# A transformer block with a feed-forward layer: both first feed-forward products as two row tiles between the score pairs, the output projection in chunks of four

## The reference

```
def _ada_rmsnorm(x, t, gamma_w, beta_w):
    return gamma * _rmsnorm(x) + beta          # gamma, beta: t @ weights, one row per sequence
def _attention(x, W_q, W_k, W_v, W_o):         # 16 heads, d_head = 16, scale = 1/4
    attn = softmax(scale * einsum('bnqd,bnkd->bnqk', q, k))
    return einsum('bnqk,bnkd->bnqd', attn, v) ... @ W_o.T
def _swiglu(x, gate_w, hidden_w, out_w, out_b):
    return silu(x @ gate_w.T) * (x @ hidden_w.T) @ out_w.T + out_b
x = x + a_alpha * _attention(_ada_rmsnorm(x, ...), ...)
x = x + f_alpha * _swiglu(_ada_rmsnorm(x, ...), ...)
out = ((x - mean) * rsqrt(var + eps) * weight + bias + tanh(convInfo @ lin_w.T + lin_b)) * weight + bias
```

## Time and profile before

| | |
|---|---|
| median of 3 runs | 820.65 us (817.95 to 827.77) |
| the profiled execution | 820.58 us, of which the span of the trace is 818.6 us |
| mean granted clock of TensorE | 0.971 of full speed (2.4 GHz) |
| busy: PE, PEld | 743.4 us (91%), 489.4 us |
| busy: DVE, ACT, POOL | 536.4 us (66%), 479.0 us (59%), 386.1 us (47%) |
| DMA | 100.15 MB, 122 GB/s in the mean |

### The profile page before, as it was taken

The page is one execution under the profiler, slowest core; times in us unless marked ns, Lnnn a source line. Parts: engine busy times, 40 slices in busy tenths (PEclk is TensorE's granted clock), DMA queues, the critical chain, the costliest instruction groups (busy, mean ns, idle before and its releaser), DMA issues.

```text
span 818.6 us, 14287 instructions
## 1 busy us (share of the span) xinstructions
PE 743.4 (91%) x5110; PEld 489.4 (60%) x5110; DVE 536.4 (66%) x777; ACT 479.0 (59%) x854; POOL 386.1 (47%) x489
## 2 busy tenths in 40 slices
PE   4767878899999999899998999899998999999896
PEld 3423333356666667566766666666675666569895
DVE  3576676667667776667666776667666677526586
ACT  3346666666656665667566666567546565663332
POOL 3234341533246542657147453656337443674753
PEclk9769999899999999999999999999999999999898
DMA  6756385244422544054421644243430630022010
GB/s 184 256 196 205 122 255 176 89 169 131 168 80 88 198 108 154 30 181 137 152 91 39 218 111 141 79 151 123 143 118 17 193 114 33 29 65 81 14 27 26
DMA packets 60670, 100.15 MB, mean 122 GB/s; under 512 B 9424, under 2 KB 17032, under 8 KB 60600
## 3 DMA queue, kind: packets, MB, share of 16 engines
q1 hardware_dynamic: 59928, 98.52, 37.6%
q10 hardware_dynamic: 544, 0.52, 0.2%
q0 software_dynamic: 128, 0.20, 0.1%
HBM read 59.60 MB, written 39.09 MB: 121 GB/s over the span
## 4 chain that ended last, share of the span: by engine, by line
PE 70%; DVE 8%; DMA 6%; issue 6%; ACT 5%; POOL 3%; SPq 1%; POOLq 0%; ACTq 0%; DVEq 0%
PE ps_x L1176 15%; PE ps_o L1156 11%; PE ps_s L1143 11%; PE ps_j L1073 11%; PE ps_x L1191 9%; PE ps_m L1128 7%; DVE mx L904 3%; ACT prob L739 3%; DMA qs<-m_hl 2%; PE ps_j L1111 1%; POOL fx L517 1%; PE ps_m L1176 1%; DVE sc L915 1%; DMA stack_scratch<-qk_lo 1%; PE ps_s L1176 1%
## 5 line engine op out<-in xcount | busy, mean ns | idle before, releaser
L904 DVE TENSOR_REDUCE mx<-ps_m 128x2 f32<-128x1024 f32 x222 | 271.8, 1224 | 88.2 <-PE ps_m L1128 83.0
L739 ACT ACTIVATE prob<-ps_s 128x1024 f32<-128x1024 f32 x256 | 262.0, 1024 | 114.6 <-PE ps_s L1143 114.0
L1143 PE MATMUL ps_s<-qs,ks 64*128 64x512 f32 x512 | 129.5, 502 | 22.3 <-ACT prob L739 12.6
L1143 PEld LDWEIGHTS ps_s<-qs,ks 64*128 64x128 f32 x512 | 48.3, 185 | 155.1 <-ACT prob L739 128.6
L1156 PE MATMUL ps_o<-prob,v 128*32 128x512 f32 x1024 | 138.3, 613 | 0.0
L482 POOL TENSOR_TENSOR a_lo<-act_y,a_hi 128x256 fp32r<-128x256 f32 x100 | 73.2, 732 | 137.0 <-ACT a_hi L771 136.4
L1176 PE MATMUL ps_x<-n_hi,gh_hi 128*128 128x256 f32 x436 | 127.3, 292 | 0.0
L1176 PE MATMUL ps_x<-n_hi,gh_lo 128*128 128x256 f32 x436 | 122.0, 280 | 0.0
L1176 PE MATMUL ps_x<-n_lo,gh_hi 128*128 128x256 f32 x436 | 121.8, 279 | 0.0
L1128 PE MATMUL ps_m<-ks,qs 64*128 64x512 f32 x444 | 100.7, 450 | 10.1 <-DVE mx L904 7.5
L764 ACT ACTIVATE gate_t<-ps_x 128x256 f32<-128x256 f32 x109 | 41.9, 384 | 93.8 <-PE ps_x L1176 93.6
(11 more groups left out here) (158 smaller groups left out, 1310.3 us busy)
## 6 DMA issues: line engine op xcount, KB each, us to landing
qs<-stack_scratch SPq DMA_DIRECT2D x32, 512.0 KB, 4.1
ks<-stack_scratch SPq DMA_DIRECT2D x32, 512.0 KB, 5.0
stack_scratch<-qk_hi SPq DMA_DIRECT2D x60, 256.0 KB, 3.2
out_scratch<-o_raw SPq DMA_DIRECT2D x32, 256.0 KB, 2.4
stack_scratch<-qk_lo SPq DMA_DIRECT2D x30, 256.0 KB, 3.6
xa<-in_x SPq DMA_DIRECT2D x8, 512.0 KB, 4.0
o_c<-out_scratch SPq DMA_DIRECT2D x16, 256.0 KB
d_c<-reciprocal_scratch SPq DMA_DIRECT2D x16, 256.0 KB
```

The costliest lines, as they stand in the source:

```text
L739: act.activation(prob[:, n % 2, 2 * h:2 * h + 2, :], ps_s[:], ACT.Exp, scale=SCALE).then_inc(p_r, 1)
L904: dve.tensor_reduce(mx[:, group % 2, :, h, qt], max_pair(mp)[:], AX.X, ALU.max).then_inc(mx_red, 1)
L1143: mm = pe.matmul(ps_s[:, s, :], ks[r:r + 64, g, j, kb * P:(kb + 1) * P], qs[r:r + 64, g, j, :], start=True, stop=True)
```

## The change

PE's order in units 28 to 127 becomes: `scores(n, 0)`, `max_scores`, `gate_hidden(e)`, `scores(n, 1)`, `max_scores`, `attend(n - 1)`, in every fourth unit a chunk, `job(n)`.

- `gate_hidden(e)` is now 24 matmuls over 64 rows and 256 columns, in twelve pairs. In a pair the upper half of the rows works for the gate channels and the lower half for the hidden channels; they write the two banks of `ps_x`. The gate weights lie in partitions 0 to 63 and the hidden weights in partitions 64 to 127 (the loads of the weights are split accordingly). Since each half of the rows must see all 256 inputs, the inputs are stored a second time with the halves of the partitions swapped (`n2_x`); SP copies them with two DMAs for each half sequence (`swap_halves`), and the seventh pair waits for them.
- `project_out` is no longer run in every unit: `project_chunk` does four values of e in a row (24 matmuls) into `ps_j`, in slots 2, 6, 10 and 14 from unit 34 on, 24 chunks in all. DVE scales each chunk and POOL adds it: twice per half sequence instead of once. The buffers of the activations grow from 4 to 6 (`RING`), and `gate_t` and `act_y` shrink by one each.
- In the units with a chunk the MT job goes to `ps_x[:, 0]` and not to `ps_j`. The next `gate_hidden` waits for its evacuation (`m_lo_r`).
- V and K change places in `SCHEDULE`. `qk_hi` and `qk_lo` have one buffer each and not two, and some of SP's issues move by one slot.
- ACT does `tanh(e)` before the second exponentials. DVE does `gate(e)` behind the two reductions, then the scaling of the chunk, then the evacuation of the job.
- In the tail PE does two `gate_hidden` and then two `project_out`, where it alternated. The products of 32 values of e are left for the tail there, and were 30.

The core of the diff:

```diff
--- before.py
+++ after.py
-SCHEDULE = (("TR", 1, 1), ("FT", 1, -2), ("MT", 1, 0), ("Q", 0, 1), ("K", 0, 1), ("V", 0, 1), ("MT", 2, 0), ("WO", 0, -1),
-            ("WO", 1, -1), ("FT", 0, -1), ("MT", 3, 0), ("Q", 1, 1), ("K", 1, 1), ("V", 1, 1), ("MT", 0, 1),
+SCHEDULE = (("TR", 1, 1), ("FT", 1, -2), ("MT", 1, 0), ("Q", 0, 1), ("V", 0, 1), ("K", 0, 1), ("MT", 2, 0), ("WO", 0, -1),
+            ("WO", 1, -1), ("FT", 0, -1), ("MT", 3, 0), ("Q", 1, 1), ("V", 1, 1), ("K", 1, 1), ("MT", 0, 1),
...
+CH = 4
+CHUNKS = TAIL // JC * JC // CH
+CHUNK_AT = GH_AT + CH + LAG
+RING = 6
+def chunk_at(n):
+
+    c = (n - CHUNK_AT) // CH
+    return c if n >= CHUNK_AT and (n - CHUNK_AT) % CH == 0 and c < CHUNKS else None
...
+        n2 = sb("n2", [P, 2, 2, KC, HT], F32R)
+        n2_x = sb("n2_x", [P, 2, 2, KC, HT], F32R)
+        gate_t = sb("gate_t", [P, HT])
...
-        ps_f = ps_x[:, 1].rearrange("p (t n) -> p t n", t=2)
+        ps_f = ps_o[:].rearrange("p (t n) -> p t n", t=2)
+        ps_c = ps_j[:].rearrange("p (t n) -> p t n", t=2)
...
+        def gh_banks(e):
+
+            return ps_x if e < TAIL else (ps_m, ps_x, ps_s)[(e - TAIL) % 3]
...
+        def mt_bank(n):
+
+            return ps_j if chunk_at(n) is None else ps_g
...
+            def swap_halves(b, h):
+
+                hf = 2 * b + h
+                sp.wait_ge(n2_lo_r, 2 * (hf + 1))
+                if b > 0:
+                    sp.wait_ge(gh_full, JC * (hf - 1))
+                for r in range(2):
+                    sp.dma_start(n2_x[64 * r:64 * r + 64, h].bitcast(F32), n2[64 - 64 * r:128 - 64 * r, h].bitcast(F32))\
+                      .then_inc(n2_x_in[h], 16)
...
             def gate_hidden(e):
 
-                hf, j, bank = e // JC, e % JC, gh_bank(e)
-                user = gh_bank_user(e)
-                if user is not None:
-                    pe.wait_ge(y_r, user + 1)
-                if e >= TAIL:
-                    pe.wait_ge(p_r, 2 * NU)
-                    pe.wait_ge(mx_red, 2 * NU)
+                hf, j, bank = e // JC, e % JC, gh_banks(e)
+                h = hf % 2
+                if gh_user(e) is not None:
+                    pe.wait_ge(y_r, gh_user(e) + 1)
                 if j == 0:
                     pe.wait_ge(n2_lo_r, 2 * (hf + 1))
                 if e == 0:
                     pe.wait_ge(piece_lo, PIECES)
                     pe.wait_ge(mx_red, 2 * (GH_AT + LEAD))
+                if e == TAIL:
+                    pe.wait_ge(p_r, 2 * NU)
+                    pe.wait_ge(mx_red, 2 * NU)
+                mt = job_at(e + GH_AT - 1)
+                if chunk_at(e + GH_AT - 1) is not None and mt:
+                    pe.wait_ge(m_lo_r, NG * mt[2] + mt[1] + 1)
                 for m in range(12):
-                    i, k, (a, c) = m // 6, m // 3 % 2, PARTS[m % 3]
-                    mm = pe.matmul(bank[:, HT * i:HT * (i + 1)], GH[a][:, k, i, j * P:(j + 1) * P], N2[c][:, hf % 2, k, :],
-                                   start=(m % 6 == 0), stop=(m % 6 == 5), skip_group_check=True)
+                    x, k, (a, c) = m // 6, m // 3 % 2, PARTS[m % 3]
+                    if m == 6 and j == 0:
+                        pe.wait_ge(n2_x_in[h], 32 * (hf // 2 + 1))
+                    for r in range(2):
+                        rows = slice(64 * r, 64 * r + 64)
+                        mm = pe.matmul(bank[:, r, 0:HT], GH[a][rows, 2 * k + (r ^ x), j * P:(j + 1) * P],
+                                       N2[x][rows, h, c, k, :], start=(m == 0), stop=(m == 11))
                 mm.then_inc(gh_full, 1)
...
+            def project_chunk(c):
+
+                job_evacuated(last[0])
+                for e in range(CH * c, CH * c + CH):
+                    project_out(e, ps_c, e == CH * c, e == CH * c + CH - 1)
+                last[0] = ("F", c)
...
+            def middle_unit(n):
+                scores(n, 0)
                 if n + LEAD < NU:
                     max_scores(2 * (n + LEAD))
-                if 0 < n <= NU:
-                    attend(n - 1)
-                if n < NU:
-                    scores(n, 1)
+                gate_hidden(n - GH_AT)
+                scores(n, 1)
                 if n + LEAD < NU:
                     max_scores(2 * (n + LEAD) + 1)
-                if n < NU:
-                    job(n)
-                if 0 <= e < NE:
-                    gate_hidden(e)
-                if 0 <= e - LAG < NE:
-                    project_out(e - LAG)
-                if n >= NU:
-                    job(n)
-
-            for n in range(LAST):
-                unit(n)
-
+                attend(n - 1)
+                if chunk_at(n) is not None:
+                    project_chunk(chunk_at(n))
+                job(n)
+
+            def tail_units(n):
+                e = n - GH_AT
+                for d in range(2):
+                    if e + d < NE:
+                        gate_hidden(e + d)
+                if n == NU:
+                    attend(n - 1)
+                job(n)
+                for d in range(CHUNKS * CH if n == NU else e - 2, e):
+                    if d < NE:
+                        project_tail(d)
+                job(n + 1)
```

More of the change, by code:

```diff
@@ L139, in build @@
         y_f = fx[:]
+        n2_hi, n2_lo = n2[:, :, 0], n2[:, :, 1]
+        first_hi, first_lo = (n2[:, :, i].rearrange("p h k n -> p h (k n)") for i in range(2))
+        zeros = sc[:].rearrange("p t n -> p (t n)")
         ps_s = ps("ps_s", [P, 2, T])
@@ L1186, in project_out, with project_tail, run @@
                     pe.wait_ge(a_tail_r, e - TAIL + 1)
-                if j == 0 and hf > 0:
-                    pe.wait_ge(sc_r, SC_NO["F", hf - 1])
                 for t in range(2):
                     for m, (a, c) in enumerate(PARTS):
-                        mm = pe.matmul(ps_f[:, t, :], A[a][:, e % 4, t * P:(t + 1) * P], OW[c][:, j, :],
-                                       start=(j == 0 and m == 0 and t == 0), stop=(j == JC - 1 and m == 2),
-                                       skip_group_check=True)
+                        mm = pe.matmul(out[:, t, :], A[a][:, e % RING, t * P:(t + 1) * P], OW[c][:, j, :],
+                                       start=(first and m == 0 and t == 0), stop=(end and m == 2), skip_group_check=True)
                 mm.then_inc(f_done, 1)
-            def run(job):
+            def project_chunk(c):
[3 more added lines that the diff above has]
+                last[0] = ("F", c)
+            def project_tail(e):
+                hf, j = e // JC, e % JC
+                if j == 0:
+                    if CH * CHUNKS == e:
+                        pe.wait_ge(o_r, NG * B)
+                    else:
+                        pe.wait_ge(sc_r, SC_NO["H", hf - 1])
+                project_out(e, ps_f, j == 0, j == JC - 1)
+            def run(job, n):
                 kind, i, b = job
@@ L1254, in job, with early_unit @@
             def job(n):
-                if job_at(n):
+                if job_at(n) and mt_bank(n) is ps_j:
                     job_evacuated(last[0])
-                    run(job_at(n))
+                    run(job_at(n), n)
                     last[0] = job_at(n)
-            def unit(n):
-                e = n - GH_AT
-                if n < NU:
-                    scores(n, 0)
+                elif job_at(n):
+                    pe.wait_ge(s_r, n - GH_AT + 1)
+                    run(job_at(n), n)
+            def early_unit(n):
+                scores(n, 0)
+                max_scores(2 * (n + LEAD))
+                if n > 0:
+                    attend(n - 1)
+                scores(n, 1)
+                max_scores(2 * (n + LEAD) + 1)
+                job(n)
+            def middle_unit(n):
+                scores(n, 0)
                 if n + LEAD < NU:
                     max_scores(2 * (n + LEAD))
-                if 0 < n <= NU:
-                    attend(n - 1)
-                if n < NU:
-                    scores(n, 1)
+                gate_hidden(n - GH_AT)
+                scores(n, 1)
                 if n + LEAD < NU:
                     max_scores(2 * (n + LEAD) + 1)
-                if n < NU:
-                    job(n)
-                if 0 <= e < NE:
-                    gate_hidden(e)
-                if 0 <= e - LAG < NE:
-                    project_out(e - LAG)
-                if n >= NU:
-                    job(n)
-            for n in range(LAST):
-                unit(n)
+                attend(n - 1)
+                if chunk_at(n) is not None:
+                    project_chunk(chunk_at(n))
[6 more added lines that the diff above has]
+                if n == NU:
+                    attend(n - 1)
+                job(n)
+                for d in range(CHUNKS * CH if n == NU else e - 2, e):
+                    if d < NE:
+                        project_tail(d)
+                job(n + 1)
+            for n in range(GH_AT):
+                early_unit(n)
+            for n in range(GH_AT, NU):
+                middle_unit(n)
```

(2 more changed lines are left out.)

277 lines of the change are left out of this document (151 added, 126 removed).

## The result

The changed kernel takes 865.7 us in the median (864.42 to 865.92, 4 runs) against 823.2 of the kernel before on the same chip: a ratio of 1.054 (1.050 to 1.058), slower. The span of its profiled execution is 863.8 us, against 818.6.

What follows compares the result with a forecast made beforehand. PE was taken to bound units 28 to 121. To 820.6 us were added 17 for those units, 12 for the tail and 1 for units 0 to 27, giving 850, with a range of 806 to 871.

Steps and rivals of the forecast that it cites:

- PE's own work, 89 to 84.1 a block, and the waits, 12.3: Block of 16 units: PE's work falls from 89 to 84.1 us, waits come to 12.3, so 96.4 against 92.7.
- my list: Waits of one block summed by the kind of job before them: 13.3 us, taken as 12.3.
- Units 28 to 121, +17: Large stage: +3.7 us a block gives +21.7 over 94 units, less 4.5 for first six units without chunks.
- Units 0 to 27, +1: Start of the kernel: same order, but K one unit later and more DMA issues, +1 us.
- Halved `qk_hi`, 0, at worst 1 a block: Q and K evacuations: a write lands in 3.2 us, two units lie between, so 0, at worst 1 us per block.
- The last six units, 0: Units 122 to 127: no max_scores, so no reduction to wait for; the groups come to the same 26 us.
- The tail, +12: Tail: tiling changes 5.6 us, two more project_out 1.4, waits for the swapped copy 5; bounds 3 and 18.
- rival 1: Large stage: evacuations behind the job stay hidden, waits stay at 3.5 us a block, 799 us, faster; chance 0.13.
- w: The waits in a block, in us, in the forecast's formula for the whole change.
- 2: Large stage: waits are about two thirds of the sum, one hiding in another, 804 to 837 us; chance 0.24.
- 3, the clock: FT in each block: granted clock falls, 7 us at half clock cost 3.4, times six, 870 us; chance 0.08.
- 4, pairs that show their loads: gate_hidden's twelve pairs: each load shows, 0.10 us, so 1.2 more per gate_hidden, about 940 us; chance 0.05.

Runs made afterwards that it cites:

- x_dve: Changed kernel, but in units 28 to 127 DVE evacuates TR, Q, K and FT jobs and takes statistics after the next unit's first reduction; 841.6 us, 1.026.
- x_job: Changed kernel with the job ahead of attend in units without a chunk, DVE's order as it was; 834.1 us, ratio 1.013.
- x_rows: Changed kernel, but SP issues the rows of the maxima ahead of the read of the stack in slots 6 and 14; 854.3 us, ratio 1.038.
- x_sched: Changed kernel with Q, K, V in the order of the kernel before; 887.9 us, ratio 1.082.
- x_full: Changed kernel with gate_hidden as twelve matmuls over all 128 rows in the same place, which changes the computation; 870.5 us, ratio 1.063.
- x_full2: x_best2 with gate_hidden as twelve matmuls over all 128 rows in the same place, which changes the computation; 832.5 us, ratio 1.015.
- x_best2: Changed kernel with DVE's and ACT's evacuations and side work deferred into the next unit, rows of maxima first on SP, chunk scaled late; 810.0 us, 0.984.

## Why the prediction was right

Direction, range and main mechanism held: 850 was forecast with 806 to 871, and 865.7 came, near the upper end of the range. The mechanism, evacuations that lost their cover and stand ahead of a reduction, is what x_dve and x_job show; x_dve puts it at 26.5 of the 45.2 us. Several sums came out well because two errors in them cancel, and that is luck. By its steps, on the profiled executions (818.6 to 863.8, +45.2; forecast +29 or 30):

- **PE's own work, 89 to 84.1 a block, and the waits, 12.3.** Means over the units 34 to 121 give 96.8 us for a block with four chunks (forecast 96.4), of which about 11.0 are waits (how much later a group starts than without a wait; as idle time the profile has 7.6 a block): 1.7 behind the TR jobs (2.7 in my list), 1.1 and 2.0 behind the FT jobs (1.1 and 2.2), 2.0 behind Q and K (2.8), 0.3 behind V (0.8), 2.0 behind the chunks (1.85), 1.9 for `fx` (1.8). So 85.8 are left for the work: 1.7 more than I summed. About 0.6 is the slower clock in slot 10, and most of the rest are loads that show behind a wait, 0.1 each, in gate_hidden (1.48 to 1.52 in eleven slots) and in max_scores. The waits came out at or under my figures but for the chunks and `fx`, which are 0.1 and a little more over them; the work came out over its figure. That the block is right to 0.4 is luck: -1.3 and +1.7. x_dve took 26.5 us from the stage and x_job 27.7, more than the 20.3 by which it had grown.
- **Units 28 to 121, +17:** +20.3. Most of the difference lies in units 28 to 33, which have no chunk yet: 3.7 a block less 4.5 makes them 3.1 shorter, and they were 0.7 shorter. The scores of unit 32 waited 1.8 us there for the rows of the maxima, and the clock fell behind that (gate_hidden 2.56 us instead of 1.51). In units 34 to 121 the errors of work and waits cancel to 0.6 us.
- **Units 0 to 27, +1:** +10.6. This is the term with the largest error. I named "K one unit later and more DMA issues" and priced it at 1, without following SP's queue: behind K's write stands the read of the stack, and behind that the rows of the maxima, for which the scores wait. That wait grew by 4.7 us and the clock fell behind it; x_rows gave back 9.1.
- **Halved `qk_hi`, 0, at worst 1 a block:** 0, but only by the swap of V and K. x_sched has it at 28 in the stage, 4.8 a block. My bound stood on "two units lie between Q and K", and that is right only for this order.
- **The last six units, 0:** +3.0. Two things: a last slot 10, unit 122, with its waits and slower clock (0.94 in the stage, have 1.00), and behind its chunk a gate_hidden which waits 0.57 because no max_scores stands between them any more. I compared sums of groups and left the waits of slots 10 and 11 out.
- **The tail, +12:** +12.6, but of other parts. Rounds are 4.61 us as forecast. The copy cost 9.4 and not 5, since I counted the waits and not the clock behind them; the change of tiling and the longer chunk cost 3.2 net and not 7, in part because the kernel before had 2.1 us of waits of its own there, for `a_lo` and `sc`, and the changed one 0.3 for `a_lo` and 0.7 for `o_raw`. The changes of tiling, priced at 5.6, are by two runs some 2.5 of it: with full-row matmuls, but the copy and its waits kept, the tail is 2.6 shorter in x_full and 2.3 in x_full2. That the sum is right is luck.
- **Slips in the sums.** 92.7 less 89 is 3.7 and not 3.5, and sixteen times 1.2 is 19.2 and not 19.7, which changes nothing. In rival 1, 5.875 x (w - 9.6) + 8.5 fits the sum of the waits before the 1 was taken off (13.3); for the 12.3 that the forecast uses it must be w - 8.6, as 84.1 + w against 92.7 gives, and then it decides at 7.2 and is faster by 2% below 4.4. The measured 11.0 is above all of these.

**The rivals.** 1 had waits of 3.5 a block and 2 about two thirds of my sum, some 8; 11.0 were there. 3, the clock, came true in part: it fell behind the FT of slot 9 in units 74 and 106, where attend and chunk took 2.8 us more together, and in unit 122. It fell in unit 58 too, but there gate_hidden took 2.56 us instead of 1.93 and the wait for the reduction behind it was shorter by as much, so it cost nothing. In units 42 and 90 it stayed at full speed. The mean of the stage is 0.98 where it was 1.00, and part of the gap to +45 is this. 4, pairs that show their loads, did not come true: the twelve pairs start 0.12 apart throughout the stage, 1.40 for all, and 1.48 to 1.52 with one load that shows. By the rule of the Trainium skill cited there (TensorE: Matmul & The Clock Gate, The mechanism), loads overlap only where the row group differs. The trace disagrees: in these pairs both row groups are busy, and no load shows but the first.

**Where the gain went.** The change holds a real gain: x_best2 takes 23 us out of the large stage, 19 of them by the tiles (x_full2). In the changed kernel the same instructions stand in an order that turns it into waits. x_best2 loses a part of it again in its longer tail (89.5 against 78.2), so the whole is a gain of 1.6% only.

**Open.** The clock: in both kernels with full-row gate_hidden the granted clock of units 28 to 121 is 1.00, in the tiled ones it is 0.97 to 1.00, with the clock at half in one place (x_job) to eight (x_sched), with or without large waits. No run here tells why.

```profile
168.70:709.00 540.30, 526.31 (x3676) 340.27 (x3675) 369.79 (x539) 331.12 (x595) 273.66 (x341) 1.00 0.41 132
176.30:745.90 569.60, 533.93 (x3676) 342.87 (x3675) 366.67 (x539) 336.97 (x595) 273.63 (x341) 1.00 0.40 125
```

The first row is x_full2, the second x_full. Not tried: an earlier FT job or copy in the tail, an FT in slot 9 that finds `fx` ready, the chunks of four against project_out in every unit, and two buffers of `qk_hi` with the order of before.
